# The graph term's identity: added by VectorE to the adjacency block, or multiplied in by TensorE

## The chip, the cores and the metric
The kernel runs on one core of a Trainium2 chip. The metric is the device time of one launch in microseconds (us). The median of three runs of the kernel before is 627.07 us (626.67 to 628.39).

## What is computed
x is 4096 x 128, adj is a dense symmetric-pattern 4096 x 4096 matrix, W is 128 x 128, all float32:

```python
h   = adj.T @ x                                  # spectral part, first product
x1  = layernorm(x + adj @ (exp(-evals * t)[:, None] * h))
A   = adj + eye(N)
out = layernorm(x1 + tanh((A / A.sum(1, keepdims=True)) @ (x1 @ W) + b))
```

The last line holds the matter of the change: (adj + I) @ (x1 W) is adj @ (x1 W) plus x1 W itself.

## The kernel before
adj is 64 MB and doesn't fit on the chip, so it is read from memory in three stages. The 4096 rows are 8 groups of 512. In stage 1 (L349 to L367, L596, L749) each group is read once and the first product is made. A float32 operand is split in two halves of a reduced type, hi and lo: ACT copies to hi (L462), VectorE (and in four places of the last group GpSimd) makes lo = raw - hi (L599, L404), and TensorE makes three products, hi*hi, lo*hi, hi*lo (L761 to L763).

Stages 2 and 3 work in 200 steps (`STEP`, L115). A step is half a block of one group (512 rows) by one unit (512 columns): 128 x 1024 elements. Its stations:
- SP and ACT issue the loads (L336), 512 KB to 1 MB, into buffers of raw (four, and two more in late_raw in stage 3). A load holds two units of one group and stays for all steps that use it.
- VectorE transposes 32 x 32 squares into vt (L616, `turn_step`), two steps ahead of the others. It waits for the load and for a free slot: vt, hi and lo are rings of six slots, and a slot is free when TensorE has done the step six before (`wait_slot`, L315).
- ACT makes hi (L476), and then GpSimd (L423), or VectorE in every fourth step and in stage 3 every tenth (L623, `on_vector`, L132), makes lo. In some steps (`whole`, L124) there is neither, and TensorE takes vt in full float32 (L781).
- TensorE multiplies (L779 to L787): for the spectral sum of the group (`acc2`), with s_hi and s_lo, and for the graph sum (`acc3`), with p = x1 W of the step's unit. Steps of a group and unit for which p is already known do both on one transposed block. The others are done for the graph sum later: the own block of a group (unit == group) always, since its p is known last.

The own block's graph steps begin at steps 46 (group 1), 80 (3), 114 (5), 134 (0), 146 (2), 150 (7), 168 (6) and 192 (4). Steps 0 to 133 are stage 2 and the others stage 3 (visit 8). Of the transposes on VectorE there is one for each step, in order, so the 80th is that of step 79.

When a group's spectral sum is done, `ending2` runs in pieces, each some steps later than the last, on all engines: ACT copies the sum (L523), TensorE transposes it (L839), VectorE adds x and takes statistics (L689, L675, L681), GpSimd makes the inverse deviation (L412 to L417), ACT normalises to x1 (L516), TensorE transposes x1 (L844), ACT reorders it to stage (L529), TensorE makes p = x1 W in four products (L850), ACT makes p_hi (L537) and VectorE p_lo (L697). With the four products goes a fifth one here, of 512 columns, that adds (x1 W) transposed to the group's graph sum (L853): that is the I of A. It opens the sum's bank for group 0 (start=True) and joins the sum elsewhere. Semaphore xw_done counts it. `ending3` does the like for the graph sum: row degrees, b, tanh, statistics, output (L549, L708, L554, L716, L675, L559).

A bank of the graph sum is free for some groups only by turns. Group 0's sum, which is x1 W alone until stage 3, is copied to saves (L539) and comes back in stage 3 through a product with the identity (L809); group 1's sum is carried the same way (L570).

The order of the work is written out: each engine runs over positions p, does step p (TensorE p - 3, VectorE's transposes p + 2), and then the pieces of the endings that fall on p. All engines wait on each other by semaphores alone.

Of the kernel before, what the change touches and what calls it, by code (L numbers as in the profile page):

```python
# [27 lines left out]
def spectral_then_graph_conv(nc, x, adj, evals, t, W, b, out):  # L28
# [17 lines left out]
    P = 128  # L46
# [103 lines left out]
    ENDINGS = sorted(range(NG), key=END3.__getitem__)  # L150
    KEPT1_END = max(s for s in range(STEPS) if STEP[s].graph and STEP[s].group == 1 and STEP[s].visit < NG)
# [3 lines left out]
    BANK3 = {0: 7, 1: 2, 2: 3, 3: 4, 4: 5, 5: 6, 6: 7, 7: 2}  # L155
# [42 lines left out]
    with ctx:  # L198
# [33 lines left out]
        saves = sb("saves", [P, 2, CW])  # L232
# [21 lines left out]
        def load_buffer(n):  # L254

            buf = LOADS[n].buf
            if buf >= BUFS:
                return late_raw[:, buf - BUFS, :]
            return raw[:, 2 * buf:2 * buf + 2].rearrange("p k r w -> p (k r w)")

# [14 lines left out]
        def columns(rows):  # L275
# [23 lines left out]
            sem, ("deg_s", "sum3", "sumT_done", "pre3", "tanh_ready", "y_ready"))  # L299
        st3, mv3, ve3, pw3, rs3, out_ready = map(sem, ("st3", "mv3", "ve3", "pw3", "rs3", "out_ready"))  # L300
# [133 lines left out]
        def _(act):  # L434
# [85 lines left out]
            def ending2(g, since):  # L520
# [12 lines left out]
                if since == 11:  # L533
                    act.wait_ge(xw_done, g + 1)
                    if g >= WHOLE_FROM:
                        nc.scalar.activation(full[:, g - WHOLE_FROM, :], acc2(g)[:, 2 * C:4 * C], ACT.Copy)
                    nc.scalar.activation(p_hi[:, g * R * C:(g + 1) * R * C], acc2(g), ACT.Copy).then_inc(phi_ready, 1)  # L537
                    if g == 0:
                        nc.scalar.activation(saves[:, 0, :], acc3(0, 0), ACT.Copy).then_inc(saved, 1)  # L539
# [22 lines left out]
            for p in range(AHEAD, POSITIONS):  # L562
# [4 lines left out]
                if p == KEPT1_END + LAG + 2:  # L567
                    act.wait_ge(mm_done, KEPT1_END + 1)
                    act.wait_ge(xw_done, 2)
                    nc.scalar.activation(saves[:, 1, :], acc3(1, 0), ACT.Copy).then_inc(saved, 1)  # L570
# [10 lines left out]
        def _(dve):  # L581
# [28 lines left out]
            def turn_step(s):  # L610
                st = STEP[s]
                if st.half == 0:
                    dve.wait_ge(block_in[LOADS[st.load].buf], landed(st.load))
                wait_slot(dve, s)
                m = 2 * st.half
                nc.vector.transpose(  # L616
                    vt[:, slot(s), :].rearrange("p (m a i) -> p m a i", m=2, a=RB),
                    load_buffer(st.load).rearrange("p (a m e i) -> p e m a i", a=RB, m=JB, e=2)
                    [:, st.unit % 2, m:m + 2]).then_inc(vturned, 1)
# [117 lines left out]
        def _(pe):  # L737
# [51 lines left out]
            def products(s):  # L789
# [4 lines left out]
                carried = st.visit == NG and g in LATE3  # L794
# [10 lines left out]
                if first3 and carried:  # L805

                    pe.wait_ge(p_ready, NG - 1 + LATE3[g])
                    pe.wait_ge(saved, LATE3[g] + 1)
                    nc.tensor.matmul(acc3(g, NG), ident[:, :], saves[:, LATE3[g], :], start=True, stop=False)  # L809
                if first3 and g == 6:  # L810
                    pe.wait_ge(saved, 1)
                if first3 and g == LAST:
                    pe.wait_ge(saved, 2)
# [21 lines left out]
            def ending2(g, since):  # L835
# [11 lines left out]
                if since == 10:  # L847
                    pe.wait_ge(x1T_ready, g + 1)
                    for m in range(JB):
                        nc.tensor.matmul(acc2(g)[:, m * C:(m + 1) * C], stage[:, 1, m * P:(m + 1) * P], w_sb[:, :],  # L850
                                         start=True, stop=True)

                    nc.tensor.matmul(acc3(g, g), w_sb[:, :], stage[:, 1, :].rearrange("c (m q i) -> c q m i", m=JB, q=QN),  # L853
                                     start=g == 0, stop=g == 0).then_inc(xw_done, 1)
# [43 lines left out]
```

## Time and profile before

| what | value |
|---|---|
| median of three runs | 627.07 us (626.67 to 628.39) |
| the profiled execution, its own time | 626.41 us |
| its span, first to last instruction | 624.5 us |
| mean granted TensorE clock | 0.981 |
| TensorE busy | 586.1 us, 94% |
| VectorE busy | 515.2 us, 82% |
| ACT busy | 400.6 us, 64% |
| GpSimd busy | 365.8 us, 59% |
| chain of waits, by engine | PE 78%, POOL 9%, DVE 5%, ACT 3% |
| chain, by line | L785 to L787 39%, L761 to L763 27%, POOL L423 7%, L781 6%, L853 1% |

The profile calls TensorE PE, VectorE DVE, ScalarE ACT, GpSimd POOL. All times of rows are us from the start of the span, or ns where it says mean ns. GpSimd's share is low over the whole because it has next to nothing to do in stage 1 (until about 200 us); stage 2 ends at about 497 us. Busy times of TensorE come from modelled ends. A timeline row stands for one instruction or for a run of the same kind (x7: seven), and its second number is the time from the start of the first to the end of the last.

### The profile page before, as it was taken

What the parts mean: (1) busy time and instruction counts of PE and PEld (TensorE: products, weight loads), DVE (VectorE), ACT (ScalarE), POOL (GpSimd) and SP (SyncE); (2) the same over time, 40 slices, a digit from 0 to 9 for tenths busy, and PEclk for the clock granted to TensorE, in tenths of its full rate; (3) what the DMA queues carried; (4) which work ended last, traced back from release to release, by engine and by line L of the source; (5) the groups of instructions that cost most, each with busy time, mean ns of one, the idle gap of its engine ahead of it and who ended that gap; (6) DMA issues with size and microseconds to landing.
All of it is one profiled execution on the core that took longest, in us unless ns stands there. A gap on an engine that the chain in (4) does not pass through costs nothing.

```text
span 624.5 us, 8078 instructions
## 1 busy us (share of the span) xinstructions
PE 586.1 (94%) x2486; PEld 453.4 (73%) x2486; DVE 515.2 (82%) x605; ACT 400.6 (64%) x860; POOL 365.8 (59%) x210
## 2 busy tenths in 40 slices
PE   5999999999985799999999999999999979999993
PEld 5888888888874566667888888888888756656661
DVE  4899999999896999798889789597777586999992
ACT  4999999999975644545665646445454445544553
POOL 0000000000131988877999999779786879895972
PEclk9999999999998799999999999999999989999997
DMA  8999999999999899999996999387996299999201
GB/s 306 409 408 407 410 409 409 409 409 409 409 260 281 222 307 261 271 271 256 317 240 178 269 267 313 85 236 207 257 243 169 79 338 329 347 337 335 54 18 50
DMA packets 125065, 174.67 MB, mean 280 GB/s; under 512 B 6884, under 2 KB 105700, under 8 KB 125032
## 3 DMA queue, kind: packets, MB, share of 16 engines
q1 hardware_dynamic: 72608, 121.68, 59.5%
q10 hardware_dynamic: 52424, 52.58, 31.1%
q8 instruction: 17, 0.28, 0.2%
q14 instruction: 16, 0.13, 0.1%
HBM read 172.13 MB, written 2.11 MB: 279 GB/s over the span
## 4 chain that ended last, share of the span: by engine, by line
PE 78%; POOL 9%; DVE 5%; ACT 3%; issue 2%; ACTq 1%; DMA 1%; DVEq 0%
PE ps L785 13%; PE ps L787 13%; PE ps L786 13%; PE ps L761 9%; PE ps L762 9%; PE ps L763 9%; POOL lo L423 7%; PE ps L781 6%; DVE vt L616 3%; PE ps L850 1%; PE ps L853 1%; PE ps L746 1%; ACTq L336 1%; POOL rstd L415 1%; ACT hi L476 1%
## 5 line engine op out<-in xcount | busy, mean ns | idle before, releaser
L423 POOL TENSOR_TENSOR lo<-vt,hi 128x1024 fp32r<-128x1024 f32 x129 | 327.4, 2566 | 57.4 <-ACT hi L476 56.5
L616 DVE STREAM_TRANSPOSE vt<-raw 128x1024 f32<-128x1024 f32 x184 | 222.3, 1226 | 64.7 <-PE ps L787 54.4
L476 ACT ACTIVATE hi<-vt 128x1024 fp32r<-128x1024 f32 x163 | 169.8, 1061 | 110.3 <-DVE vt L616 91.8
L599 DVE TENSOR_TENSOR lo<-raw,hi 128x1024 fp32r<-128x1024 f32 x124 | 155.5, 1257 | 17.1 <-ACT hi L462 7.9
L462 ACT ACTIVATE hi<-raw 128x512 fp32r<-128x512 f32 x256 | 159.0, 624 | 5.4 <-PE ps L763 2.4
L404 POOL TENSOR_TENSOR lo<-raw,hi 128x1024 fp32r<-128x1024 f32 x4 | 10.7, 2674 | 177.0 <-ACT hi L462 177.0
L785 PE MATMUL ps<-hi,s_hi 128*128 128x512 f32 x232 | 99.0, 427 | 9.7 <-issue 5.2
L761 PE MATMUL ps<-hi,xg_hi 128*128 128x512 f32 x256 | 100.2, 392 | 2.4 <-DVE lo L599 1.8
L762 PE MATMUL ps<-lo,xg_hi 128*128 128x512 f32 x256 | 99.6, 389 | 0.0
L763 PE MATMUL ps<-hi,xg_lo 128*128 128x512 f32 x256 | 99.6, 389 | 0.0
L785 PE MATMUL ps<-hi,p_hi 128*128 128x512 f32 x206 | 89.1, 433 | 5.4 <-POOL lo L423 5.4
L786 PE MATMUL ps<-lo,s_hi 128*128 128x512 f32 x232 | 91.4, 394 | 0.0
L787 PE MATMUL ps<-hi,s_lo 128*128 128x512 f32 x232 | 91.4, 394 | 0.0
L787 PE MATMUL ps<-hi,p_lo 128*128 128x512 f32 x206 | 81.0, 393 | 0.0
L786 PE MATMUL ps<-lo,p_hi 128*128 128x512 f32 x206 | 80.9, 393 | 0.0
L781 PE MATMUL ps<-vt,full 128*128 128x512 f32 x148 | 69.5, 592 | 0.0
L623 DVE TENSOR_TENSOR lo<-vt,hi 128x1024 fp32r<-128x1024 f32 x34 | 65.3, 1920 | 1.6 <-ACT hi L476 1.6
L785 PEld LDWEIGHTS ps<-hi,s_hi 128*128 128x128 f32 x232 | 44.2, 190 | 26.1 <-issue 9.4
L761 PEld LDWEIGHTS ps<-hi,xg_hi 128*128 128x128 f32 x256 | 48.1, 188 | 13.9 <-DVE lo L599 2.3
L763 PEld LDWEIGHTS ps<-hi,xg_lo 128*128 128x128 f32 x256 | 48.1, 188 | 10.1
L762 PEld LDWEIGHTS ps<-lo,xg_hi 128*128 128x128 f32 x256 | 48.1, 188 | 9.6
L785 PEld LDWEIGHTS ps<-hi,p_hi 128*128 128x128 f32 x206 | 39.0, 189 | 21.0 <-POOL lo L423 10.2
(66 smaller groups left out, 515.9 us busy)
## 6 DMA issues: line engine op xcount, KB each, us to landing
raw<-in_adj_dram SPq DMA_DIRECT2D x63, 1024.0 KB, 14.7
raw<-in_adj_dram SPq DMA_DIRECT2D x90, 512.0 KB, 9.4
raw<-in_adj_dram ACTq DMA_DIRECT2D x88, 512.0 KB, 11.5
late_raw<-in_adj_dram SPq DMA_DIRECT2D x8, 512.0 KB, 11.3
late_raw<-in_adj_dram ACTq DMA_DIRECT2D x8, 512.0 KB, 13.5
xn<-in_x_dram SPq DMA_DIRECT2D x8, 256.0 KB, 14.4
x_sb<-in_x_dram SPq DMA_DIRECT2D x8, 256.0 KB, 13.3
out_dram<-x_sb ACTq DMA_DIRECT2D x7, 256.0 KB, 3.1
```

Of the source, the lines that this page charges most:

```text
L423: nc.gpsimd.tensor_tensor(lo[:, slot(p), :], vt[:, slot(p), :], hi[:, slot(p), :].bitcast(f32), ALU.subtract).then_inc(pool_lo_ready, 1)
L462: last = nc.scalar.activation(hi[:, q % RING1, e * CW:(e + 1) * CW], raw[:, k, 2 * h + e, :], ACT.Copy, accum_out=rsum[:, v, column:column ...
L476: nc.scalar.activation(hi[:, slot(s), :], vt[:, slot(s), :], ACT.Copy).then_inc(hi_ready, 1)
L599: nc.vector.tensor_tensor(lo[:, q % RING1, :], raw[:, k, 2 * h:2 * h + 2, :].rearrange("p r n -> p (r n)"), hi[:, q % RING1, :].bitcast(f3 ...
L616: nc.vector.transpose(vt[:, slot(s), :].rearrange("p (m a i) -> p m a i", m=2, a=RB), load_buffer(st.load).rearrange("p (a m e i) -> p e m ...
L761: nc.tensor.matmul(bank, xh, ah, start=first and r == 0, stop=False)
L762: nc.tensor.matmul(bank, xh, al, start=False, stop=False)
L763: last = nc.tensor.matmul(bank, xl, ah, start=False, stop=final and r == R - 1)
L781: return nc.tensor.matmul(out_t, full[:, STEP[s].unit - WHOLE_FROM, jj * C:(jj + 1) * C], vt[:, slot(s), jj * CW:(jj + 1) * CW], start=sta ...
L785: nc.tensor.matmul(out_t, vh, ah, start=start, stop=False)
L786: nc.tensor.matmul(out_t, vh, al, start=False, stop=False)
L787: return nc.tensor.matmul(out_t, vl, ah, start=False, stop=stop)
```

## The change
VectorE adds ones to the 512 diagonal elements of a group's own block, in its raw buffer, before the first graph step of that block. In the buffer a partition quarter q (32 partitions) holds its part of the diagonal as four 32 x 32 squares, so it takes one add of 32 x 128 elements for each quarter, with the matching 32 x 32 square of ident, repeated four times, as the other operand: four adds a group, 32 in all. Then VectorE waits for its own adds (own_ready) and goes on to the transpose. The blocks' spectral steps are done before, on the untouched data, and the next reader of the buffer comes after a new load. The product L853 goes, with it the copy of group 0's sum (L539) and its way back (L809 for group 0). Group 0's graph sum opens with its first product in stage 3. xw_done now comes with the last of the four products L850. The list of places in which the sum of group 1 is waited for changes its count.

```diff
+    OWN = [s for s in range(STEPS) if STEP[s].graph and STEP[s].unit == STEP[s].group and STEP[s].half == 0]
...
-    BANK3 = {0: 7, 1: 2, 2: 3, 3: 4, 4: 5, 5: 6, 6: 7, 7: 2}
+    BANK3 = {1: 2, 2: 3, 3: 4, 4: 5, 5: 6, 6: 7, 7: 2}
...
-        saves = sb("saves", [P, 2, CW])
+        saves = sb("saves", [P, CW])
...
+        def own_diagonal(s, q):
+            first = q * R * WQ + STEP[s].group % 2 * QP
+            flat, pitch = load_buffer(STEP[s].load)[q * QP:(q + 1) * QP], WQ + 2 * QP
+            if first + JB * pitch <= R * NU * WQ:
+                return flat[:, first:first + JB * pitch].rearrange("p (m w) -> p m w", w=pitch)[:, :, :QP]
+            end = first + (JB - 1) * pitch + QP
+            return flat[:, end - JB * pitch:end].rearrange("p (m w) -> p m w", w=pitch)[:, :, pitch - QP:]
...
+        own_ready = sem("own_ready")
...
-                    if g == 0:
-                        nc.scalar.activation(saves[:, 0, :], acc3(0, 0), ACT.Copy).then_inc(saved, 1)
...
-                    act.wait_ge(xw_done, 2)
-                    nc.scalar.activation(saves[:, 1, :], acc3(1, 0), ACT.Copy).then_inc(saved, 1)
+                    nc.scalar.activation(saves[:, :], acc3(1, 0), ACT.Copy).then_inc(saved, 1)
...
                 wait_slot(dve, s)
+                if s in OWN:
+                    for q in range(QN):
+                        block = own_diagonal(s, q)
+                        ones = ident[q * QP:(q + 1) * QP, q * QP:(q + 1) * QP].unsqueeze(1).to_broadcast([QP, JB, QP])
+                        last = nc.vector.tensor_tensor(block, block, ones, ALU.add)
+                    last.then_inc(own_ready, 1)
+                    dve.wait_ge(own_ready, OWN.index(s) + 1)
                 m = 2 * st.half
                 nc.vector.transpose(
...
-                carried = st.visit == NG and g in LATE3
+                carried = first3 and st.visit == NG and g == 1
...
-                if first3 and carried:
+                if first3 and st.visit == NG and g in LATE3:
                     pe.wait_ge(p_ready, NG - 1 + LATE3[g])
-                    pe.wait_ge(saved, LATE3[g] + 1)
-                    nc.tensor.matmul(acc3(g, NG), ident[:, :], saves[:, LATE3[g], :], start=True, stop=False)
-                if first3 and g == 6:
+                if carried:
                     pe.wait_ge(saved, 1)
+                    nc.tensor.matmul(acc3(g, NG), ident[:, :], saves[:, :], start=True, stop=False)
                 if first3 and g == LAST:
-                    pe.wait_ge(saved, 2)
+                    pe.wait_ge(saved, 1)
...
-                        nc.tensor.matmul(acc2(g)[:, m * C:(m + 1) * C], stage[:, 1, m * P:(m + 1) * P], w_sb[:, :],
-                                         start=True, stop=True)
-
-                    nc.tensor.matmul(acc3(g, g), w_sb[:, :], stage[:, 1, :].rearrange("c (m q i) -> c q m i", m=JB, q=QN),
-                                     start=g == 0, stop=g == 0).then_inc(xw_done, 1)
+                        last = nc.tensor.matmul(acc2(g)[:, m * C:(m + 1) * C], stage[:, 1, m * P:(m + 1) * P], w_sb[:, :],
+                                                start=True, stop=True)
+                    last.then_inc(xw_done, 1)
```

## Rows read from the trace of the kernel before

**Rows 1.** Windows: us; busy of PE, PEld, DVE, ACT, POOL (instructions); clock; DMA share; GB/s.

```profile
326.00:359.00 33.00, 33.00 (x152) 26.98 (x151) 29.05 (x31) 20.08 (x27) 32.84 (x16) 1.00 0.78 211
401.00:488.00 87.00, 87.00 (x397) 71.74 (x396) 63.30 (x62) 42.23 (x57) 68.61 (x34) 1.00 0.77 200
488.00:526.00 38.00, 33.41 (x134) 24.31 (x133) 25.35 (x28) 18.92 (x27) 33.12 (x18) 0.96 0.89 270
526.00:560.00 34.00, 33.40 (x123) 22.14 (x123) 31.84 (x50) 17.62 (x25) 32.00 (x21) 1.00 1.10 333
560.00:598.00 38.00, 37.82 (x132) 23.61 (x131) 36.75 (x65) 19.83 (x31) 28.34 (x22) 1.00 0.60 180
```

**Rows 2.** Waits of the whole run: waiter <- releaser: us in total, times, longest.

```profile
DVE vt L616 <- PE ps L787: 55.1, 58, 3.2
...
PE ps L785 <- POOL lo L423: 9.6, 11, 2.7
```

**Rows 3.** The chain of waits in order of time: start, us, what.

```profile
485.71 0.86 PE ps L853 x2
...
497.49 0.86 PE ps L809 x2
```

**Rows 4.** Timeline of steps 75 to 80: start, us, engine, line, operation [idle before <-releaser].

```profile
348.75 18.57 POOL L423 TENSOR_TENSOR lo<-vt,hi 128x1024 fp32r<-128x1024 f32 x7
...
352.21 1.25 DVE L616 STREAM_TRANSPOSE vt<-raw 128x1024 f32<-128x1024 f32 x1 [0.19 <-PE ps L787]
...
356.02 1.02 PE L853 MATMUL ps<-stage,w_sb 128*128 128x512 f32 x2
356.91 0.50 PE L785 MATMUL ps<-hi,s_hi 128*128 128x512 f32 x1
...
358.40 0.39 PE L785 MATMUL ps<-hi,s_hi 128*128 128x512 f32 x1
```

**Rows 5.** Timeline of the beginning of stage 3, steps 138 to 150.

```profile
507.00 0.50 PE L785 MATMUL ps<-hi,p_hi 128*128 128x512 f32 x1 [2.65 <-POOL lo L423]
...
514.20 21.19 POOL L423 TENSOR_TENSOR lo<-vt,hi 128x1024 fp32r<-128x1024 f32 x9
...
514.38 2.53 DVE L616 STREAM_TRANSPOSE vt<-raw 128x1024 f32<-128x1024 f32 x2 [1.17 <-PE ps L787]
...
530.74 0.50 PE L785 MATMUL ps<-hi,p_hi 128*128 128x512 f32 x1
```

**Rows 6.** Groups by line (count | busy us, mean ns | idle before), then single timeline rows.

```profile
L599 DVE TENSOR_TENSOR lo<-raw,hi 128x1024 fp32r<-128x1024 f32 x124 | 155.5, 1257 | 17.1 <-ACT hi L462 7.9
...
L675 DVE BATCH_NORM_STATS2 stats<-ps 128x6 f32<-128x128 f32 x64 | 13.8, 272 | 0.0
...
L593 DVE TENSOR_TENSOR xg_lo<-xn,xg_hi 128x512 fp32r<-128x512 f32 x8 | 5.5, 686 | 2.0 <-ACT xg_hi L448 2.0
...
288.43 5.75 POOL L423 TENSOR_TENSOR lo<-vt,hi 128x1024 fp32r<-128x1024 f32 x2 [0.66 <-ACT hi L476]
288.75 3.16 DVE L623 TENSOR_TENSOR lo<-vt,hi 128x1024 fp32r<-128x1024 f32 x1
...
590.77 0.85 DVE L675 BATCH_NORM_STATS2 stats<-ps 128x6 f32<-128x128 f32 x4
...
593.78 2.40 POOL L423 TENSOR_TENSOR lo<-vt,hi 128x1024 fp32r<-128x1024 f32 x1
```

**Rows 7.** Timeline around step 168.

```profile
552.83 4.61 DVE L616 STREAM_TRANSPOSE vt<-raw 128x1024 f32<-128x1024 f32 x4
...
555.23 7.08 POOL L423 TENSOR_TENSOR lo<-vt,hi 128x1024 fp32r<-128x1024 f32 x3
...
560.48 0.79 PE L785 MATMUL ps<-hi,p_hi 128*128 128x512 f32 x1
```

**Rows 8.** Timeline around step 192.

```profile
591.95 4.73 DVE L616 STREAM_TRANSPOSE vt<-raw 128x1024 f32<-128x1024 f32 x4
...
600.07 0.79 PE L785 MATMUL ps<-hi,p_hi 128*128 128x512 f32 x1
```

## The prediction

> **What bounds the kernel now.** I read the table of windows first, because the whole-span shares mix three stages. TensorE (PE) is busy without a hole in the stretches of stage 2 shown (326 to 359, 401 to 488 us), and almost so from 526 to 598; the stretch with holes is 488 to 526, with 33.41 us of 38 [rows 1]. So TensorE work taken out pays only where nothing else is due just then. GpSimd (POOL), which makes most of the lo halves, is as full as TensorE from 326 to 359 (32.84 us of 33) and from 526 to 560, and has room from 401 to 488. VectorE (DVE) has room until 526 and none from 560 to 598 (36.75 of 38) [rows 1]. What waits there tell: TensorE waits on GpSimd's lo (9.6 us over the run), VectorE on TensorE for a free ring slot (55.1 us); no transpose waits for a load [rows 2]. The ring of six slots closes the circle: a transpose of step s+6 waits for the products of step s, then come hi, lo and the products.
>
> **What is removed.** The product of x1 and W into the graph accumulator (L853) leaves two records for each of the 8 groups; the chain of waits puts 0.86 us on the pair, and as much on the pair of group 0's carry (L809) [rows 3]. Nine pairs are 7.7 us. Which of them are on the path:
> - Groups 0 and 1 (ahead of the full stretch): the endings and lo's behind them are paced by TensorE, and both count, 1.7 us.
> - Groups 2 and 3: GpSimd is full in 326 to 359. Step 77's products start at 356.91 just behind L853 (356.02). Seven lo's run from 348.75 without a hole [rows 4]; at 2.40 us each and 1 us more for the one that meets VectorE's lo (below), the third ends at 356.9. Without L853 TensorE waits for it instead. These two give nothing.
> - Groups 4, 5, 6 (the last at 485.71): TensorE alone is full from 401 to 488 [rows 1, 3]. All count, 2.6 us.
> - Group 7 (in the stretch from 514) and the carry (497.49): TensorE waits 2.65 us for lo at 507.00, and from 514.20 nine lo's run without a hole, to 535.39 [rows 3, 5]. Nothing.
> The sum is 4.3 us. ACT loses one copy and one wait on xw_done; p_hi is released a pair sooner. These lie beside other work and I count nothing.
>
> **What is added.** Eight times, ahead of the first transpose of the own block (steps 46, 80, 114, 134, 146, 150, 168, 192), VectorE does four adds of 32 partitions by 128 elements, and then a semaphore wait. Size: 128x1024 takes 1257 ns and 128x512 takes 686 ns where GpSimd is idle [rows 6], so the slope is 1.12 ns an element and 128 elements come to 0.26 us. Bounds are 0.21 us (L675, 128 elements, four in 0.85) and 0.69 us (the 128x512) [rows 6]. I take 0.26, and for four with the wait 1.2 us. Behind the adds on VectorE's queue stand the transpose, the lo that VectorE makes itself, and the endings' operations; ACT waits for the transpose and GpSimd for ACT. No DMA is added or moved. A buffer comes free some us later; as no transpose waits for a load now, I count nothing for it.
>
> **The dear part is a shared resource.** VectorE's lo of 1024 elements takes 1257 ns in stage 1, almost all of it without GpSimd at work (L599). In stage 2 the one at 288.75 takes 3.16 us; beside it GpSimd does two operations from 288.43 in 5.75 us, 1.0 more than two at the 2.40 us of one alone [rows 6]. So an operation of two SBUF operands on one engine waits out the other engine's whole operation, and the one that waited goes first when it ends.
>
> Four adds in a row meet this four times. If GpSimd's next lo waits when an add ends, it goes first, and the next add waits 2.40 us. I take this case. That no row has two such VectorE operations in a row with a GpSimd one waiting keeps its price open: between 0 and 2.40 us for each add.
>
> Does one VectorE operation leave GpSimd a hole before the next? Four L675 of 272 ns each take 0.85 us together, so the next one starts before the last one ends [rows 6]. All of these start in partition 0.
>
> The Trainium skill (VectorE: DVE Perf Modes, "Two Vector instructions with no wait between them") says that a VectorE instruction whose start quadrant differs from the last one's starts only when all earlier ones are done. By that rule the four adds, in four quadrants, have a hole after each, GpSimd gets in, and the time is the forecast's; with the overlap that L675 shows it could be the second rival's. No row here shows a change of quadrant.
>
> Step by step, with alternation:
> - Step 80. VectorE is ready at 352.21 [rows 4]. GpSimd's lo of step 76 ends at 353.54; add; lo of 77 to 356.2; add; lo of 79 to 358.9; two adds (step 80's lo isn't ready); transpose to 360.8; then VectorE's own lo of step 78, to 362.0. TensorE starts step 78 at 358.40 now. Late by 3.6 us.
> - Steps 146 and 150. Ready at 514.38; GpSimd in step 142's lo to 516.6; add; 144's to 519.2; three adds; transpose 146 from 520.2, two more, lo of 146 done at 525.0. Transposes 148 and 149 end at 525. The next adds meet the lo's of 147, 148, 149 (to 527.4, 530.1, 532.8); transpose 150 ends at 534.7, hi at 535.8, lo at 538.2. TensorE starts step 150 at 530.74 now [rows 5]. Late by 7.5 us.
> - Step 168. The transpose stands in the run from 552.83, at 554.0. Ahead is GpSimd's lo from 555.23, the first of three without a hole. Between 0 and 3.0 us (the adds drawn out behind that lo, transpose done at 559.9, lo at 563.5; TensorE starts at 560.48 now) [rows 7]; I take half, 1.5.
> - Step 192. VectorE is at 593.1 (the second transpose of the run from 591.95), GpSimd's lo starts at 593.78 [rows 6]. Between 0 and 1.7 us, since VectorE's own lo of this step slides behind that one, to end at 601.8, and TensorE starts the step at 600.07 now [rows 8]; I take 0.9.
> - Steps 46, 114, 134. VectorE waits for free slots around them (114 lies in 401 to 488, where it is busy 63.30 us of 87), and TensorE has lo's in hand there, as it never stops [rows 1]. Nothing, at most 0.7 us.
> The sum is 3.6 + 7.5 + 1.5 + 0.9 - 4.3 = +9.2 us. On the profiled execution (626.41 us, its span 624.5) that is 635.6 us. It stands 0.66 us under the median of 627.07 us, so the forecast for the median is 636.3 us. After 526 TensorE has about 1 us of holes left, so a stall there isn't won back [rows 1].
>
> **Rivals.**
> 1. *Alternation* (the forecast): slower, 636.3 us, with 632 to 642 from the bounds. It decides where GpSimd has two or more lo's ready as VectorE reaches an own block, which steps 80, 146 and 150 have.
> 2. *The four adds go as one.* VectorE holds the port across them. One wait of up to 2.40 us and 1.2 us of adds. Step 80's own lo chain then ends at 358.2, just in time, but GpSimd comes 1.2 us late in the full stretch; at 146 and 150 the lo of 150 ends at 533.4, 2.7 us late; 0.3 us for 192. -4.3 + 1.2 + 2.7 + 0.3 = -0.1: 627.0 us. For it: VectorE, when waiting, did win at 288.75. Against it: by the same rows GpSimd's second operation went first when VectorE's ended.
> 3. *The adds are too small to contend* (32 partitions, 128 elements). Then 1.2 us on VectorE each time, covered in stage 2 and worth some 0.5 us where VectorE is full: -3.8, 623.3 us. Against it: no row shows an exempt operation of two SBUF operands.
> 4. *TensorE's whole 7.7 us count*: 619.4 us. GpSimd's full stretches speak against it.
>
> **How the numbers follow.** Within 0.3% is 1.9 us, about what a measurement can tell from no change. Alternation 0.58: 0.51 slower, 0.05 the same, 0.02 faster. As one 0.20: 0.04 slower, 0.11 the same, 0.05 faster. Too small 0.17: 0.15 faster, 0.02 the same. Everything counts 0.05, faster. Together 0.27 faster, 0.18 the same, 0.55 slower. The range goes from 622 (the third case and a bit) to 641 (alternation with most upper bounds); alternation's own is 632 to 642.
>
> **What would show it.** Right: add records of 2.4 us and more, with GpSimd lo's of 2.4 us between them, a gap of several us before the transposes of steps 80, 146 and 150, and new TensorE idle time released by lo behind these, 11 us or so. L853 and two L809 records gone. Stage 2 up to step 77 ends 1.7 us earlier. Wrong: the four adds of a block together under 4 us with GpSimd busy; then case 2 or 3, told apart by the first add's length (1.2 us in the mean, or 0.26). TensorE waiting on VectorE's own lo less than 1 us at step 78 would take 3.6 us from the sum.

## The result, and the profile after

The changed kernel takes 638.92 us (median of four runs, 638.39 to 639.97) against 626.87 us for the kernel before (four runs, 625.44 to 628.39): a ratio of 1.0216 with a 95% interval of 1.0195 to 1.0237. That is 12.1 us slower, where 9.2 us was forecast; 638.92 lies in the range. Three of the kernels below had one execution each of 1002.91 to 1514.98 us, which is left out of their ratios and of the medians given here. The profiled execution took 639.25 us, its span 637.4 us (626.41 and 624.5 before).

The page: busy time by engine, and the chain of waits by engine.

```profile
PE 584.5 (92%) x2468; PEld 451.0 (71%) x2468; DVE 549.9 (86%) x637; ACT 400.1 (63%) x859; POOL 365.5 (57%) x210
...
PE 66%; DVE 13%; POOL 11%; issue 4%; ACT 4%; ACTq 1%; DMA 1%; DVEq 0%
```

TensorE is busy only 1.6 us less, by the modelled ends, with 18 matmuls less (2468 for 2486); VectorE is busy 34.7 us more, for which the 32 adds alone (35.6 us, below) would do. On the chain TensorE fell from 78% to 66%, and VectorE rose from 5% to 13%.

The table of windows, to be laid beside [rows 1] (the columns are the same; the second window is new, and the last one reaches to 610 here).

```profile
326.00:359.00 33.00, 31.33 (x143) 25.02 (x141) 31.28 (x31) 16.48 (x23) 31.97 (x16) 1.00 0.74 200
359.00:368.00 9.00, 6.98 (x24) 5.59 (x25) 8.53 (x8) 5.78 (x6) 6.97 (x3) 0.81 0.51 124
401.00:488.00 87.00, 87.00 (x404) 72.56 (x403) 70.68 (x68) 42.39 (x56) 68.39 (x34) 1.00 0.73 200
488.00:526.00 38.00, 30.70 (x129) 23.44 (x128) 30.70 (x35) 17.02 (x25) 28.54 (x16) 0.96 0.84 255
526.00:560.00 34.00, 29.38 (x106) 19.18 (x105) 32.26 (x41) 15.41 (x21) 28.23 (x16) 0.95 1.02 272
560.00:610.00 50.00, 48.99 (x166) 29.74 (x165) 48.01 (x86) 24.65 (x40) 38.11 (x30) 1.00 0.69 189
```

From 401 to 488 TensorE is as full as before, and does seven matmuls more (404 against 397): there the removed products came back as time. The holes lie where they were forecast: 7.3 us from 488 to 526 (4.6 before), 4.6 us from 526 to 560 (0.6 before) and some 3.7 us around 359. The granted clock is 0.81 around 359 and 0.95 from 526 (1.00 before); the prediction had nothing on that.

Waits and one group of the whole run, against [rows 2] and the bounds of [rows 6].

```profile
DVE vt L633 <- PE ps L804: 35.0, 39, 2.6
...
PE ps L802 <- POOL lo L436: 16.9, 14, 4.0
...
PE ps L802 <- DVE lo L640: 4.0, 2, 3.6
...
PE ps L802 <- DVE p_lo L714: 2.5, 1, 2.5
```

```profile
L629 DVE TENSOR_TENSOR raw<-raw,ident 32x128 f32<-32x128 f32 x32 | 35.6, 1113 | 4.7 <-PE ps L804 4.4
```

TensorE's waits on GpSimd's lo grew from 9.6 to 16.9 us. A wait of 3.6 us on VectorE's own lo is new (step 78), and the one on VectorE's p_lo (group 0) grew from 0.4 to 2.5 us. VectorE waits 20 us less for ring slots; its spare time went into the adds. An add takes 1113 ns in the mean. The shortest take 236 to 289 ns; 11 of the 32 take 2.3 to 2.5 us.

Steps 77 to 80, to be read beside [rows 4] (the first VectorE row is the first of the block's four adds alone, the second all four).

```profile
351.93 1.56 DVE L629 TENSOR_TENSOR raw<-raw,ident 32x128 f32<-32x128 f32 x1 [0.19 <-PE ps L804]
...
351.93 6.65 DVE L629 TENSOR_TENSOR raw<-raw,ident 32x128 f32<-32x128 f32 x4 [0.19 <-PE ps L804]
...
353.31 2.44 POOL L436 TENSOR_TENSOR lo<-vt,hi 128x1024 fp32r<-128x1024 f32 x1
...
355.71 2.42 POOL L436 TENSOR_TENSOR lo<-vt,hi 128x1024 fp32r<-128x1024 f32 x1
...
358.61 1.25 DVE L633 STREAM_TRANSPOSE vt<-raw 128x1024 f32<-128x1024 f32 x1
359.78 1.18 DVE L640 TENSOR_TENSOR lo<-vt,hi 128x1024 fp32r<-128x1024 f32 x1
...
355.80 0.50 PE L802 MATMUL ps<-hi,s_hi 128*128 128x512 f32 x1
...
361.02 0.50 PE L802 MATMUL ps<-hi,s_hi 128*128 128x512 f32 x1 [3.57 <-DVE lo L640]
...
362.55 0.63 PE L802 MATMUL ps<-hi,s_hi 128*128 128x512 f32 x1
```

The four adds take 1562, 2391, 2371 and 289 ns. The first three each end 0.15 us after one of GpSimd's lo's has ended (353.3, 355.7, 358.1), and the fourth finds GpSimd without one ready. The transpose comes at 358.6, VectorE's lo of step 78 ends at 361.0, and TensorE has stood for 3.57 us: the forecast had 358.9 and two adds, then 362.0. Then the clock falls: a matmul of 512 columns takes 0.63 us at 362.55 (0.39 just before), as the granted clock is 0.5 (1.2 GHz) from 362.47 to 365.88.

The beginning of stage 3, beside [rows 5].

```profile
516.53 5.33 DVE L629 TENSOR_TENSOR raw<-raw,ident 32x128 f32<-32x128 f32 x4 [1.51 <-PE ps L804]
521.89 4.62 DVE L633 STREAM_TRANSPOSE vt<-raw 128x1024 f32<-128x1024 f32 x4
526.44 7.56 DVE L629 TENSOR_TENSOR raw<-raw,ident 32x128 f32<-32x128 f32 x4
534.03 2.37 DVE L633 STREAM_TRANSPOSE vt<-raw 128x1024 f32<-128x1024 f32 x2
...
524.31 9.54 POOL L436 TENSOR_TENSOR lo<-vt,hi 128x1024 fp32r<-128x1024 f32 x4 [3.19 <-ACT hi L489]
...
538.85 0.50 PE L802 MATMUL ps<-hi,p_hi 128*128 128x512 f32 x1 [3.29 <-POOL lo L436]
```

Step 146's adds lose two turns (2328, 2384, 283, 289 ns) and step 150's three (395, 2376, 2373, 2377 ns), as forecast: GpSimd's lo's of steps 146 to 149 run from 524.31 to 533.85, the first add of step 150 meets only the tail of the first of them, and the other adds wait out one each. Step 150 starts at 538.85 instead of 530.74. From 539.97 to 543.38 the granted clock is 0.5 again.

**Where the time went.** Take the start of TensorE's first product of a step, in the trace after minus in the trace before, and call it the offset of that step (a subtraction of timeline rows). It tells stretch by stretch what was lost. It is -2.18 us at step 0: this execution had come through stage 1, which the change doesn't touch, faster. From there to step 199 the offset grows by 15.1 us, of which the two medians show 12.1.

| stretch (steps) | offset at its end | gained in it | forecast |
|---|---|---|---|
| 0 to 36 (group 0) | +0.7 | +2.9 | -0.86 (half of 1.7) |
| 36 to 77 (groups 1, 2, 3) | -1.1 | -1.8 | -0.86 |
| 77 to 84 (adds of step 80) | +4.4 | +5.5 | +3.6 |
| 84 to 130 (groups 4, 5, 6; adds of 114) | +1.7 | -2.7 | -2.6 |
| 130 to 144 (adds of 134; carry) | +2.1 | +0.4 | 0 |
| 144 to 156 (adds of 146, 150; group 7) | +9.8 | +7.6 | +7.5 |
| 156 to 186 (adds of 168) | +10.5 | +0.8 | +1.5 |
| 186 to 199 (adds of 192) | +12.9 | +2.4 | +0.9 |

Of the +7.6 in the row of steps 146 and 150, 6.0 us are there when step 150 starts (8.1 of offset against 2.1 at step 144); the other 1.6 us come behind that, at the lower clock level. The first row has the wrong sign. At step 30 (group 0's p is due there) the two traces read as follows; first the kernel before.

```profile
256.09 0.59 ACT L539 ACTIVATE saves<-ps 128x512 f32<-128x512 f32 x1
...
258.48 1.18 DVE L623 TENSOR_TENSOR lo<-vt,hi 128x1024 fp32r<-128x1024 f32 x1
259.59 0.68 DVE L697 TENSOR_TENSOR p_lo<-ps,p_hi 128x512 fp32r<-128x512 f32 x1
...
258.66 5.65 POOL L423 TENSOR_TENSOR lo<-vt,hi 128x1024 fp32r<-128x1024 f32 x2 [1.16 <-ACT hi L476]
...
260.41 0.47 PE L785 MATMUL ps<-hi,s_hi 128*128 128x512 f32 x1 [0.39 <-DVE p_lo L697]
```

And the kernel after:

```profile
250.64 10.40 POOL L436 TENSOR_TENSOR lo<-vt,hi 128x1024 fp32r<-128x1024 f32 x4 [0.91 <-ACT hi L489]
...
255.46 3.35 DVE L640 TENSOR_TENSOR lo<-vt,hi 128x1024 fp32r<-128x1024 f32 x1
258.73 0.68 DVE L714 TENSOR_TENSOR p_lo<-ps,p_hi 128x512 fp32r<-128x512 f32 x1
...
259.55 0.47 PE L802 MATMUL ps<-hi,s_hi 128*128 128x512 f32 x1 [2.54 <-DVE p_lo L714]
260.53 0.63 PE L802 MATMUL ps<-hi,p_hi 128*128 128x512 f32 x1
```

Before, VectorE's lo got in 0.18 us ahead of GpSimd's (258.48 against 258.66). After, GpSimd is in a lo already, since 255.34, 0.12 us before VectorE comes to its own; VectorE's takes 3.35 us in place of 1.18, p_lo stands behind it on the queue, and TensorE idles 2.54 us and then runs at the lower clock level from 260.07 to 263.49: 3.7 us in all (2.89 and the 0.84 of the removed pair). No add is near: the first stands at step 46. ScalarE's copy L539 just before is gone, and so ACT's next hi starts 0.50 us after the start of p_hi (252.57, 253.07) and not 0.97 us after it (255.60, 256.57); GpSimd's lo's wait for these hi's.

### The profile page after: what moved, and what is told of

Its sections match the earlier page's. It is cut to its first block, busy times and chain, and to the rows that moved or that the text cites. A ratio compares the mean times of both kernels' runs of the same rounds, so it can differ in the third digit from the quotient of the medians.

```text
span 637.4 us, 8071 instructions
## 1 busy us (share of the span) xinstructions
PE 584.5 (92%) x2468; PEld 451.0 (71%) x2468; DVE 549.9 (86%) x637; ACT 400.1 (63%) x859; POOL 365.5 (57%) x210
## 4 chain that ended last, share of the span: by engine, by line
PE 66%; DVE 13%; POOL 11%; issue 4%; ACT 4%; ACTq 1%; DMA 1%; DVEq 0%
PE ps L802 11%; PE ps L804 11%; PE ps L803 11%; POOL lo L436 9%; PE ps L778 9%; PE ps L780 9%; PE ps L779 9%; DVE vt L633 6%; PE ps L798 4%; DVE raw L629 4%; ACT hi L489 1%; ACTq L349 1%; PE ps L763 1%; DVE stats L692 1%; POOL rstd L428 1%
## 5 line engine op out<-in xcount | busy, mean ns | idle before, releaser
L798 PE MATMUL ps<-vt,full 128*128 128x512 f32 x148 | 70.9, 602 | 0.0
L640 DVE TENSOR_TENSOR lo<-vt,hi 128x1024 fp32r<-128x1024 f32 x34 | 66.6, 1958 | 3.7 <-ACT hi L489 3.7
L802 PEld LDWEIGHTS ps<-hi,s_hi 128*128 128x128 f32 x232 | 44.5, 192 | 31.4 <-issue 10.5
```

Of the source, the lines that this page charges most:

```text
L798: return nc.tensor.matmul(out_t, full[:, STEP[s].unit - WHOLE_FROM, jj * C:(jj + 1) * C], vt[:, slot(s), jj * CW:(jj + 1) * CW], start=sta ...
L802: nc.tensor.matmul(out_t, vh, ah, start=start, stop=False)
```

## The experiments

Ratios are to the kernel before, run on the same chip beside it, with 95% intervals. "Trace" is the growth of the offset from step 0 to step 199 of each one's trace (15.1 us for the changed kernel), which leaves out what stage 1 did. Diffs are against the changed kernel, unless they say otherwise.

**The changed kernel without its adds** (the removals alone, so the identity is missing from its result).

```diff
-                if s in OWN:
...
-                    last.then_inc(own_ready, 1)
-                    dve.wait_ge(own_ready, OWN.index(s) + 1)
```

> The changed kernel without its 32 adds (so the identity is missing from the graph product): only TensorE's work is taken out. Theory A (the changed kernel's trace: VectorE's lo of step 31, moved 0.86 us earlier by the missing product of group 0, now begins behind GpSimd's lo instead of ahead of it, takes 3.35 us, and holds up p_lo of group 0; TensorE then stands 2.5 us at step 30 and runs some us at the half clock): this costs 3.8 us and eats most of the gain, ratio to the kernel before 0.998 (626 us), and the idle row of 2.5 us at step 30 is there. Theory B (the prediction: the taken-out work of groups 0, 1, 4, 5, 6 counts in full): 622.6 us, ratio 0.993, no such idle row.

Measured: 627.57 us, 1.0035 [1.0014, 1.0056]; trace +2.8 us. The adds are most of the loss, but what is left is no gain at all; both forecasts of the ratio missed, the nearer one (0.998) too, though its stall at step 30 is there. Group 0's stall is there unchanged, the turn lost at step 30 included.

```profile
358.54 0.50 PE L795 MATMUL ps<-hi,s_hi 128*128 128x512 f32 x1 [0.80 <-POOL lo L436]
```

That is step 77: with L853 gone TensorE waits for GpSimd's lo there, as forecast for groups 2 and 3. The stretch from 36 to 84 gave 0.7 us, about group 1's pair alone. The 2.6 us of groups 4 to 6 are there. What that theory lacked lies in stage 3. The carry's pair gives 0.9 us at step 134, and 1.3 us is gone again by step 144; group 7's pair gives 0.9 us at step 145, and that is gone by step 150. Between steps 156 and 160, 1.5 us is lost behind VectorE's lo of step 156: GpSimd's lo starts at 536.10 and VectorE's at 536.16, which then takes 3.41 us and so holds up the next transpose (before, VectorE's starts at 536.77 and takes 1.18 us, GpSimd's at 537.07). It is a second turn lost by a shift of tenths. Another 1.2 us is lost from step 170 to 182; what loses it was not isolated.

**The kernel before with 32 adds of zeros** (all of the removed work is back; the diff is against the kernel before, own_diagonal and OWN are as in the change).

```diff
...
+                if s in OWN:
+                    dve.wait_ge(nought_ready, 1)
+                    for q in range(QN):
+                        block = own_diagonal(s, q)
+                        ones = nought[q * QP:(q + 1) * QP, :].unsqueeze(1).to_broadcast([QP, JB, QP])
+                        last = nc.vector.tensor_tensor(block, block, ones, ALU.add)
+                    last.then_inc(own_ready, 1)
+                    dve.wait_ge(own_ready, OWN.index(s) + 1)
```

> The kernel before plus the 32 adds, of zeros, at the places of the change; TensorE's products all stay. Theory A (adds alternate with GpSimd's lo operations: terms read from the changed kernel's trace, 4.6 us at step 80, 7.6 at 146 and 150, 0.5 at 168, 2.4 at 192): +15 us, 642 us, ratio 1.024, mean of an add 1.1 us. Theory B (the adds cost their bare 1.2 us for each group and the changed kernel's loss is mostly another's): +3 us or less, ratio under 1.006.

Measured: 640.06 us, 1.0246 [1.0217, 1.0275]; trace +15.3 us. Group 0's stall is absent (the offset doesn't move from step 0 to 36), and groups 4 to 6 gain nothing. The adds cost 4.6 us from step 36 to 84 (1.7 of it after step 78 has begun, at the lower clock level), 7.7 us from 144 to 156 (again 6.0 of it up to the start of step 150, and 1.7 behind that, at the lower level), 1.7 from 156 to 168 and 1.3 after that.

**One add of 128 x 512 elements in place of the four.**

```diff
-                    for q in range(QN):
...
-                    last.then_inc(own_ready, 1)
+                    flat = load_buffer(st.load)
+                    block = bass.AP(flat.tensor, flat.offset + st.group % 2 * QP,
+                                    [list(flat.ap[0]), [R * WQ, QN], [WQ + 2 * QP, JB], [1, QP]])
+                    ones = ident[:, :].rearrange("p (q i) -> p q i", q=QN).unsqueeze(2).to_broadcast([P, QN, JB, QP])
+                    nc.vector.tensor_tensor(block, block, ones, ALU.add).then_inc(own_ready, 1)
```

It touches four times as many columns on all partitions (off the diagonal it adds zeros), and gives the same sum.

> The changed kernel with one add of 128 partitions x 512 elements for each own block instead of four of 32 x 128 (the rest of ident is zeros, so the result is the same). More elements and 0.69 us instead of 4 x 0.28 us bare. Theory A (each separate operation loses one turn to GpSimd): an add takes 0.7 to 3.1 us, steps 80 and 150 lose at most 1 and 3 us instead of 4.6 and 7.6, and the kernel comes to 627 to 631 us, some 10 us under the changed one. Theory B (the loss goes with the elements moved through the shared port, or with a VectorE that is too full): no better than the changed kernel, 636 us or more.

```profile
L630 DVE TENSOR_TENSOR raw<-raw,ident 128x512 f32<-128x512 f32 x8 | 13.0, 1630 | 4.4 <-PE ps L804 4.2
```

Measured: 628.74 us, 1.0048 [1.0029, 1.0068]; trace +4.5 us. A block now has one add, and it loses one turn at most: it takes 1.97 us at step 80 and 2.72 us at 146, and 0.65 to 0.69 us where it meets no lo. More work in fewer operations costs 10 us less. So what costs is the number of times that VectorE asks, not the elements.

**Four adds, all on partitions 0 to 31** (each quarter of the columns in turn).

```diff
-                        block = own_diagonal(s, q)
-                        ones = ident[q * QP:(q + 1) * QP, q * QP:(q + 1) * QP].unsqueeze(1).to_broadcast([QP, JB, QP])
+                        e = STEP[s].group % 2
+                        block = load_buffer(st.load)[0:QP, q * R * WQ + e * P:q * R * WQ + (e + 1) * P].rearrange("p (m w) -> p m w", w=QP)
+                        ones = ident[0:QP, 0:QP].unsqueeze(1).to_broadcast([QP, JB, QP])
```

> The changed kernel with its four adds all on partitions 0 to 31 (wrong elements get the ones, so the diagonal of three quarters is missing). Same count and size, but no change of start quadrant between them. Theory A (GpSimd, when it waits, goes first after each VectorE operation, whatever the quadrant): adds of 2.4 us as in the changed kernel, 638 to 640 us. Theory B (only the hole that a change of quadrant leaves lets GpSimd in): the four adds go as one, one wait of up to 2.4 us, none of the later three over 0.3 us, and 628 to 632 us.

```profile
353.84 6.54 DVE L630 TENSOR_TENSOR raw<-raw,ident 32x128 f32<-32x128 f32 x4 [0.19 <-PE ps L805]
...
567.26 0.85 DVE L630 TENSOR_TENSOR raw<-raw,ident 32x128 f32<-32x128 f32 x4
```

Measured: 639.58 us, 1.0212 [1.0184, 1.0239], the changed kernel's ratio. The turns are lost one by one without any change of quarter (1544, 2469, 2462, 273 ns at step 80). Without GpSimd near, at step 168, four take 0.85 us here against 1.13 us in the changed kernel: within one quarter of the partitions an add starts some 0.2 us after the last, before that one has ended, and when the quarter changes 0.25 to 0.30 us after it, once it has ended. The Trainium skill states such a hold (VectorE: DVE Perf Modes, "Two Vector instructions with no wait between them"): a VectorE instruction that starts in another quadrant than the last one starts only when the earlier ones have finished. The trace agrees with it. But it isn't what lets GpSimd in, as the prediction's working by that rule had it, for the time and the lost turns are the same without it.

**The adds as operations of one operand** (statistics of the same size).

```diff
...
-                        block = own_diagonal(s, q)
...
-                        last = nc.vector.tensor_tensor(block, block, ones, ALU.add)
+                        block = load_buffer(st.load)[q * QP:(q + 1) * QP, q * R * WQ:q * R * WQ + P]
+                        last = nc.vector.bn_stats(own_stats[q * QP:(q + 1) * QP, :], block)
```

> The changed kernel with its 32 adds replaced by 32 statistics operations that read one SBUF operand of the same 32 x 128 elements (the identity is missing from the graph product). Count, size, quadrants and the wait behind them stay; only the second SBUF operand goes. Theory A (the second SBUF operand makes an operation take turns with GpSimd): none of the 32 over 0.35 us, and the time is that of the kernel without adds plus at most 1.5 us, 628 to 630 us. Theory B (four short operations and a wait on VectorE's queue cost this much by themselves): 636 us or more.

```profile
L629 DVE BATCH_NORM_STATS2 own_stats<-raw 32x6 f32<-32x128 f32 x32 | 9.0, 281 | 4.7 <-PE ps L804 4.4
```

Measured: 627.80 us, 1.0031 [1.0014, 1.0048]; trace +2.8 us, as with no adds at all. Not one takes over 291 ns, at the same places and with GpSimd in its lo's as before (at step 80 from 349.18 to 356.31, while these four run from 352.55 to 353.73). They also write less than an add does, 6 elements a partition for 128; but VectorE's transposes, which write all that they read and have one operand, aren't drawn out by a lo either (1.25 us at 350.49 in the changed kernel, with GpSimd in its lo's from 348.57 to 358.12). So the price hangs on the second operand in SBUF. The Trainium skill (SBUF — State Buffer, "SBUF: two separate sides") describes it as an exclusive lock for whole instructions between a VectorE operation with two SBUF inputs and a GpSimd operation that reads SBUF. The runs agree, 281 against 1113 ns.

**The changed kernel with group 0's product back, its result unused.**

```diff
+                    if g == 0:
+                        last = nc.tensor.matmul(ps[:, 7, :], w_sb[:, :], stage[:, 1, :].rearrange("c (m q i) -> c q m i", m=JB, q=QN),
+                                                start=True, stop=True)
```

> The changed kernel with one product of 512 columns given back to TensorE behind group 0's four (into an unused bank, the result isn't read), so TensorE does 0.86 us more. Theory A (without it VectorE's lo of step 31 begins behind GpSimd's lo instead of ahead of it and holds up p_lo of group 0): that lo takes 1.2 us again, TensorE's 2.5 us of idle time at step 30 and the half clock behind it are gone, and the kernel is 2 to 3 us FASTER than the changed one, 636 us. Theory B (that stall isn't due to the order of these two): as the changed kernel or 0.9 us slower, 639 to 640 us.

```profile
256.65 5.71 POOL L436 TENSOR_TENSOR lo<-vt,hi 128x1024 fp32r<-128x1024 f32 x2 [0.68 <-ACT hi L489]
...
256.96 3.16 DVE L640 TENSOR_TENSOR lo<-vt,hi 128x1024 fp32r<-128x1024 f32 x1
```

Measured: 640.83 us, 1.0242 [1.0218, 1.0266]; trace +13.2 us. A miss: TensorE still waits 2.35 us at step 30, since GpSimd's lo is again the first, by 0.31 us. The product alone doesn't bring the order back.

**The changed kernel with ScalarE's copy back**, into a tile that nobody reads; first with the product of the last experiment, then alone.

```diff
...
+                    if g == 0:
+                        nc.scalar.activation(spare[:, :], ps[:, 7, :], ACT.Copy)
```

> The changed kernel with both of group 0's missing pieces given back where they stood, the product of 512 columns and ACT's copy of 128 x 512 from its bank behind p_hi (the copy's result isn't read). Theory A (the earlier run, with the product alone, still lost the turn: its GpSimd lo began at 256.65 and VectorE's at 256.96, since without ACT's copy of 0.59 us the hi's come early): VectorE's lo of step 31 takes 1.2 us, TensorE stands 0.4 us instead of 2.5 at step 30, and the kernel is 2.9 us faster than the changed one, 636 us. Theory B (something else of the change makes that stall): 639 to 641 us, 2.4 to 2.5 us of idle time at step 30.

> The changed kernel with ACT's copy alone given back behind p_hi of group 0. Theory A (ACT's copy sets the order; in the changed kernel's trace 0.5 us more on ACT would put GpSimd's lo at 255.6, behind VectorE's at 255.46): no stall at step 30, 3.7 us faster than the changed kernel, 635 us, though it does more work. Theory B (product and copy are both needed): the stall stays, 639 us.

The copy alone:

```profile
257.34 1.18 DVE L643 TENSOR_TENSOR lo<-vt,hi 128x1024 fp32r<-128x1024 f32 x1
...
257.51 5.64 POOL L437 TENSOR_TENSOR lo<-vt,hi 128x1024 fp32r<-128x1024 f32 x2 [0.27 <-ACT hi L490]
...
259.27 0.47 PE L805 MATMUL ps<-hi,s_hi 128*128 128x512 f32 x1 [0.38 <-DVE p_lo L717]
```

Measured: 637.10 us, 1.0185 [1.0160, 1.0210] with both, and 636.67 us, 1.0191 [1.0162, 1.0219] with the copy alone; traces +12.3 and +10.9 us. Either way VectorE's lo is first by 0.17 us, and the stall is gone; the copy does it. The two intervals overlap with the changed kernel's, so times alone would not have shown it. The traces do: for the copy alone the offset is 3.8 us better by step 31 and 4.2 us by step 199. By the ratios it is 1.6 us where 3.7 us were forecast. With the product there too, without and with the copy, the intervals lie apart (1.0218 to 1.0266, and 1.0160 to 1.0210).

**The kernel before with that copy about 40 us later**, beside group 1's (diff against the kernel before): the same work with another place for one operation of 0.6 us.

```diff
-                    if g == 0:
-                        nc.scalar.activation(saves[:, 0, :], acc3(0, 0), ACT.Copy).then_inc(saved, 1)
...
+                    nc.scalar.activation(saves[:, 0, :], acc3(0, 0), ACT.Copy).then_inc(saved, 1)
                     nc.scalar.activation(saves[:, 1, :], acc3(1, 0), ACT.Copy).then_inc(saved, 1)
```

> The kernel before with one thing moved: ACT's copy of group 0's sum (L539, 0.59 us) stands next to group 1's copy, some 40 us later, so the work is the same and the result too. Theory A (this copy is what kept GpSimd's lo behind VectorE's at step 31: 258.66 against 258.48 in the trace of before, and 0.5 us less on ACT turns it round): VectorE's lo takes 3.2 to 3.4 us, TensorE stands 2.3 to 2.6 us at step 30 with a stretch at the half clock behind it, and the kernel is 3 to 4.5 us slower, ratio 1.005 to 1.007. Theory B (the stall in the changed kernel needs its other edits): the time of the kernel before, ratio 1.000.

```profile
258.01 5.69 POOL L423 TENSOR_TENSOR lo<-vt,hi 128x1024 fp32r<-128x1024 f32 x2 [0.67 <-ACT hi L476]
...
258.32 3.15 DVE L622 TENSOR_TENSOR lo<-vt,hi 128x1024 fp32r<-128x1024 f32 x1
...
262.22 0.76 PE L784 MATMUL ps<-hi,s_hi 128*128 128x512 f32 x1 [2.36 <-DVE p_lo L696]
```

Measured: 627.86 us, 1.0033 [1.0019, 1.0048]; trace +3.9 us, of which 3.5 us between steps 27 and 31 and nothing more until step 144. This settles the cause at group 0: in the kernel before, the copy held ACT just long enough for VectorE to go first. It doesn't settle the size. Four pairs of kernels here differ by this copy alone. In the traces the kernel with the copy in its place is 3.4 to 3.8 us ahead at step 31 in each. By the ratios it is 1.6 us (the changed kernel), 3.6 us (with the product), 2.1 us (with one wide add, 1.0048 and 1.0015) and 2.1 us (this one, under its forecast of 1.005 or more). Most of these allow some 2 us either way, but here the interval ends at 3.0 us; the traced execution is the slowest of its eight. Whether the turn is lost in every execution is not shown, since one was traced of each kernel.

**What can be had.** Three versions with the one wide add: for groups 1, 4, 5 and 6 alone, with the products, the copy and the carry of the others as before; for groups 0, 1, 4, 5 and 6, with the copy kept as a mere delay; and for all eight, with the copy. The second's diff, beside the wide add:

```diff
-    OWN = [s for s in range(STEPS) if STEP[s].graph and STEP[s].unit == STEP[s].group and STEP[s].half == 0]
+    OWN = [s for s in range(STEPS) if STEP[s].graph and STEP[s].unit == STEP[s].group and STEP[s].half == 0
+           and STEP[s].group in (0, 1, 4, 5, 6)]
...
+                    if g == 0:
+                        nc.scalar.activation(spare[:, :], ps[:, 7, :], ACT.Copy)
...
+                    if g in (2, 3, 7):
+                        last = nc.tensor.matmul(acc3(g, g), w_sb[:, :], stage[:, 1, :].rearrange("c (m q i) -> c q m i", m=JB, q=QN),
+                                                start=False, stop=False)
```

> The kernel before, with the identity of groups 1, 4, 5 and 6 alone added by VectorE, in one add of 128 x 512 elements each, and the product kept for groups 0, 2, 3 and 7, whose loss or whose own block (steps 80, 134, 146, 150) costs or gives nothing. Theory A (where a product's end lies on TensorE's path and the own block meets idle GpSimd or waiting time, 0.86 us each is a net gain; group 0's order is left alone): 3.4 us less, ratio 0.994 to 0.996; if VectorE's lo of step 156 also loses its turn, as in the three experiments before, 1.5 us of it goes, ratio 0.997. Theory B (any change of when TensorE ends shifts some VectorE lo behind a GpSimd one and costs as much): 1.000 or more.

> As the kernel with four groups (1, 4, 5, 6 in one add each; 0.9977 of the kernel before), and group 0 too: its product, its carry and its way back are gone, ACT's copy is kept for its time. Products stay for groups 2, 3 and 7. Theory A (another 0.86 us of TensorE's path and no stall at step 30): 0.9 to 1.3 us less than that kernel, ratio 0.995 to 0.997. Theory B (group 0's own block at step 134 or a lost turn elsewhere eats it): 0.998 or more.

> The changed kernel with one add of 128 x 512 elements for each own block and with ACT's copy given back. The kernel with one add alone was 1.0048 of the kernel before. Theory A (the stall at step 30 is cured by the copy whatever else is done): 3.7 us less than that, 625 us, ratio 0.999. Theory B (the two repairs don't add up, since a cured stall moves some other VectorE lo behind a GpSimd one): 1.003 or more.

Measured, in that order: 624.21 us, 0.9977 [0.9961, 0.9992], trace -1.0; 623.19 us, 0.9973 [0.9959, 0.9987], trace -1.8; 626.11 us, 1.0015 [1.0001, 1.0030], trace +1.1. The first (forecast 0.994 to 0.997) and the second (0.995 to 0.997) come out just above their forecasts. The third misses its 0.999: in its trace it is 3.8 us ahead at step 130 and loses 4.9 us from there. The five-group version beats both kernels, by 0.3% over the one before; the four-group version can't be told from it. It keeps the products where TensorE's time isn't the limit (2, 3, 7) and so has no adds at the blocks of steps 80, 146 and 150. At step 156 it stands 3.3 us ahead in its trace, counted from step 0; from 156 to 168 it loses 1.2 us again.

## Why the prediction was right, and where it wasn't

- **The bound, and which products count.** Right. Groups 4 to 6: -2.6 forecast, -2.7 measured, and none in the run that kept them. Groups 2 and 3: nothing forecast, and with the adds out TensorE waited 0.80 us for GpSimd's lo at step 77 instead. In the changed kernel itself TensorE came 1.0 us sooner to step 77 for them, and the stall at 78, whose end VectorE sets, took it. Group 7: 0 forecast, and with the adds out its pair gave 0.9 us that was gone again five steps later. The carry: 0 forecast, +0.4 us of loss measured up to step 144, also with the adds out; the four-group version, which keeps the carry, loses 0.8 us there, so the carry isn't its cause, which stayed open.
- **Groups 0 and 1, "both count, 1.7 us".** This is the step that failed. Group 1 gave 0.86 us. Group 0's pair gave 0.84 us, and the copy of group 0's sum, of which the prediction said "these lie beside other work and I count nothing", had a price of its own: without it 3.7 us are lost at step 30. It lay beside other work, but it timed when GpSimd asked for the port, against a margin of 0.18 us that stood in the trace before. +2.9 us in place of -0.86. The sign that the prediction gave, stage 2 up to step 77 ending 1.7 us earlier, failed with it: stage 1 aside, step 77 starts 1.1 us later. By the ratios the copy is worth 1.6 to 3.6 us, as said above.
- **Alternation.** Right as a mechanism: each add waits out one lo wherever GpSimd has one ready. Steps 146 and 150: 7.5 forecast, 7.6 measured (7.7 with the adds alone). That the two agree so well is luck: step 150 starts 6.0 us late, stage 1 and all before aside, and 1.6 us is the lower clock level behind it. Step 78: the forecast's 3.6 was how late it starts against before (362.0 for 358.40). It starts at 361.02, 2.6 us late; the 3.57 us is the idle time there, another quantity, and its likeness to 3.6 is luck too. Over the steps 36 to 78 the offset rose by 1.9 us where -0.86 and 3.6 make 2.7: VectorE came to the adds at 351.93, 0.28 us earlier than before, while TensorE stood 0.7 us later at step 36. The working left open whether a change of start quadrant is what lets GpSimd in between two adds; it isn't, as one quadrant gave the same time.
- **The clock after a stall.** Not in the prediction: 1.7 us behind step 78, 1.6 behind step 150, some 1.6 of the 3.7 at step 30, 4.9 us in all. The forecast priced stalls at their idle time only.
- **Step 168**: 1.5 taken, four adds of 1.13 us together and 0.8 us in the stretch, in the bounds; the adds met no lo, and some 0.5 us of the 0.8 (steps 178 to 182) goes in the run without adds too. **Step 192**: 0.9 taken with 1.7 as the upper bound, 2.4 measured. One add of 2385 ns there as thought, but TensorE waits at step 192 (0.44 us) and again behind it (1.20 us at 623.05, for GpSimd's lo). **Steps 46, 114, 134**: 0, right, though 114's adds took 7.5 us: VectorE had the room and TensorE never stopped from 401 to 488.
- **The rivals.** "The four adds go as one" falls by the records of one block: three waits, not one. "Too small to contend" falls by the same; only the operations of one operand escaped. "The whole 7.7 us counts" falls by the removal alone, 1.0035.
- **The sum**: +9.2 forecast, +12.1 by the medians, +15.1 by the traces from step 0. Of the 5.9 us between forecast and traces group 0 is 3.8 (2.9 and 0.86) and step 80's stretch 1.9, nearly all of it the clock; the rest nearly cancels (step 192 +1.5, groups 2 and 3 -1.0, step 168 -0.7, 130 to 144 +0.4; at 146 and 150, -1.5 in the adds and +1.6 by the clock). Of the 3.0 us between medians and traces 2.2 is stage 1 of the profiled execution. TensorE's first product of step 0 came at 203.9 to 206.2 us in the traces, and what sets that stayed open. With 15.1 us on the 627.07 the time would have been 642.2 us, just over the range, so that it lies within is in part luck.

## What to carry to other kernels

Where VectorE and GpSimd both work on operands in SBUF, count VectorE's two-operand operations, not their elements: each can cost a whole operation of GpSimd, so make one wide operation of several narrow ones, or use a form with one operand (statistics and transposes were the ones seen to escape here). Before removing or moving even a half-microsecond operation from an engine off the critical path, look in the trace for pairs whose order it decides by a few tenths of a us; if what is removed holds such an order, keep it or something in its place. And take work off the bounding engine only in the stretches in which it alone is full.

## What was unexpected of the hardware

- The engines take turns by whole operations, for each size tried: an add of 32 x 128 elements takes 0.24 to 0.29 us by itself and up to 2.5 us beside GpSimd's lo of 128 x 1024, which takes 2.4 us; one of 128 x 512 takes 0.65 to 0.69 us and up to 2.9 us.
- TensorE's granted clock was 0.5 (1.2 GHz) for 3.4 us after a stall of 3.57 us, with matmuls of 512 columns at 0.63 us for 0.39 before. It isn't the same each time: in the run with the copy alone the granted clock stayed at 1.0 (355 to 368) after the same stall of 3.57 us at step 78, and 0.3 us was lost from there to step 84, against 1.7 us in the changed kernel and in four others with stalls of 2.8 to 3.6 us there. What makes the difference was not tried.
- The order of two operations that stood 0.18 us apart was worth 3.5 us in the trace (1.0033, 2.1 us, by the runs) for the same work.
